# A fused normalisation, attention and 4-bit feed-forward kernel: unit 1's ramps moved into ScalarE's pauses, operand 6 made third, eight staging slots late in the first half, and ScalarE casting in the odd steps

## What is computed

```
q     = transpose(xn, (2, 0, 1))                       # 1024 positions, 4 x 1024
prob  = softmax(einsum('lnc,lmc->lnm', q, q) / sqrt(C))  # a 4 x 4 matrix for each position
s     = xn + transpose(einsum('lnm,lmc->lnc', prob, q))
gate  = xn @ Wg.T ; up = xn @ Wu.T                     # Wg, Wu: 2752 x 1024, 4-bit codes, a scale for every 64
g     = silu((silu(gate) * up) @ Wd.T)                 # Wd: 1024 x 2752
out   = x + s * g
```

## Time and profile before

| | |
|---|---|
| time, median of three runs | 2548.71 us |
| the profiled execution's own time | 2553.62 us |
| its span | 2551.5 us |
| TensorE (PE) busy, of the span | 2427.7 us, 95% |
| VectorE (DVE) busy | 1647.6 us, 65% |
| ScalarE (ACT) busy | 992.2 us, 39% |
| mean granted clock of TensorE | 0.978 of full |
| bytes by DMA, mean rate | 579.52 MB, 227 GB/s |

### The profile page before, as it was taken

The page is one execution under the profiler, slowest core; times in us unless marked ns, Lnnn a source line. Parts: engine busy times, 40 slices in busy tenths (PEclk is TensorE's granted clock), DMA queues, the critical chain, the costliest instruction groups (busy, mean ns, idle before and its releaser), DMA issues.

```text
span 2551.5 us, 30326 instructions
## 1 busy us (share of the span) xinstructions
PE 2427.7 (95%) x11214; PEld 1112.5 (44%) x11214; DVE 1647.6 (65%) x2866; ACT 992.2 (39%) x1261; POOL 84.1 (3%) x72
## 2 busy tenths in 40 slices
PE   2789999999999989999999999999999999999999
PEld 2334444444444434444444444444444444444444
DVE  8878887778988866787888886654532431431431
ACT  7776766766666434444455522111000001000001
POOL 0000000000000000000000000000011001011011
PEclk6889999999999999999999999999999999999999
DMA  7666665756656587655556654227876777777764
GB/s 249 214 192 219 212 200 197 225 168 235 232 193 221 183 318 242 225 180 198 194 197 203 215 182 154 106 79 284 349 281 274 302 290 287 276 280 291 313 261 161
DMA packets 171855, 579.52 MB, mean 227 GB/s; under 512 B 17632, under 2 KB 42896, under 8 KB 153916
## 3 DMA queue, kind: packets, MB, share of 16 engines
q1 hardware_dynamic: 136716, 289.21, 33.5%
q10 hardware_dynamic: 34992, 288.37, 30.0%
HBM read 388.76 MB, written 188.75 MB: 226 GB/s over the span
## 4 chain that ended last, share of the span: by engine, by line
PE 75%; DVE 10%; DMA 7%; issue 4%; ACT 2%; SPq 1%; POOL 0%; DVEq 0%; POOLq 0%; ACTq 0%
PE ps L1700 44%; PE ps L1846 30%; DMA arena<-xnsc 2%; DMA isc<-arena 2%; DVE arena L1325 2%; DMA arena<-in_x 2%; DVE arena L1204 1%; DVE arena L1318 1%; DVE arena L1229 1%; ACT arena L731 1%; PE ps L1657 1%; DVE arena L1495 0%; DVE arena L1490 0%; DMA xsc<-arena 0%; DVE arena L1253 0%
## 5 line engine op out<-in xcount | busy, mean ns | idle before, releaser
L1700 PE MATMUL ps<-arena 128*128 128x512 f16 x7152 | 1574.2, 383 | 67.8 <-DVE arena L1229 23.8
L1700 PEld LDWEIGHTS ps<-arena 128*128 128x128 f16 x7152 | 703.6, 99 | 925.7 <-issue 57.8
L1846 PE MATMUL ps<-arena 128*128 128x512 f16 x3696 | 797.9, 379 | 0.0
L731 ACT ACTIVATE arena<-arena,bias_t 128x1024 f32<-128x1024 f32 (+1 forms) x520 | 574.4, 1142 | 39.5 <-DMA arena<-in_gu 24.5
L1846 PEld LDWEIGHTS ps<-arena 128*128 128x128 f16 x3696 | 361.7, 98 | 436.1
L1325 DVE TENSOR_TENSOR arena<-arena 128x512 f16<-128x512 f32 x364 | 248.6, 684 | 22.5 <-ACT arena L884 20.7
L932 ACT ACTIVATE arena<-ps,gate_back 128x512 f32<-128x512 f32 x84 | 57.5, 684 | 370.2 <-PE ps L1700 370.1
L1116 ACT ACTIVATE arena<-arena,e_d 128x512 f32<-128x512 f32 x48 | 34.6, 721 | 424.3 <-DVE arena L1622 219.4
L1318 DVE CAST arena<-arena 128x512 f16<-128x512 f32 x336 | 137.0, 420 | 53.5 <-DMA isc<-arena 47.3
L696 POOL TENSOR_TENSOR arena<-arena 128x512 f32<-128x512 f32 x64 | 82.1, 1292 | 2454.3 <-DMA arena<-in_xt 2151.7
L942 ACT ACTIVATE arena<-arena,gate_back 128x512 f32<-128x512 f32 x84 | 60.5, 721 | 239.5 <-DVE arena L1492 231.0
(11 more groups left out here) (110 smaller groups left out, 1095.1 us busy)
## 6 DMA issues: line engine op xcount, KB each, us to landing
isc<-arena SPq DMA_DIRECT2D x308, 256.0 KB, 2.3
arena<-wdsc ACTq DMA_DIRECT2D x28, 2816.0 KB, 10.2
arena<-isc ACTq DMA_DIRECT2D x28, 2816.0 KB, 18.0
arena<-xnsc SPq DMA_DIRECT2D x48, 1024.0 KB, 10.8
wsc<-arena ACTq DMA_DIRECT2D x21, 1792.0 KB, 6.4
arena<-in_x SPq DMA_DIRECT2D x48, 512.0 KB, 6.0
arena<-in_gu ACTq DMA_DIRECT2D x43, 512.0 KB, 4.5
wdsc<-arena SPq DMA_DIRECT2D x77, 256.0 KB, 2.1
```

The source lines that it names most:

```text
L731: a_.activation(buf, src, ACT.Prelu, bias=bias_t[:, i:i + 1], scale=scale, alpha=alpha).then_inc(ramps, 1)
L1700: ins = t_.matmul(ps[:, bank, :], wreg[:, b, w, wa, k, :], xreg[:, j, o, k, xa, :], start=start and (k, wa, xa) == (0, 0, 0), stop=stop an ...
L1846: ins = t_.matmul(ps[:, bank, :], ring_w[b][:, k, wa, g, :], ring_i[b][:, k, xa, :], start=first and (k, wa, xa) == (0, 0, 0), stop=r not ...
```

## The change

1. `W_ORDER` becomes 0, 4, 5, 6, 1, 3, 2 (operand 6 third of the sums and fourth of the operands); the down weights keep the old order as `D_ORDER`. `W_CUT[13]` moves one low part from slot 2 to slot 1 and the two sums from slot 3 to slot 2.
2. Unit 1's 16 ramps: six before the first normalisations on ScalarE (three before), one behind them, one or three between the casts of blocks 0, 1 and 2, one before `p1_copy(0)` and three behind it. Unit 2's stand between the casts of blocks 4 to 7, with six in step 2; unit 3's are spread over steps 2 and 3 as 4 and 12.
3. VectorE makes unit 1's weights before `early_made(4)`, around the second half of step 0. Block 4's casts go from VectorE to ScalarE.
4. Steps 40 to 46 use eight staging slots; the four more lie in the memory of the x jobs' blocks and wait until the last x job is through.
5. In the odd steps 25 to 39 ScalarE does all seven casts of the job, of i jobs too, after `p1_copy` and the weight casts, and VectorE's items are the eleven `ACT_ITEMS`, none in slot 0.
6. `STAT_AT` puts 5, 1, 4 and 4 statistics into steps 4, 5, 6 and 7 (5, 0, 6, 3 before).

The diff holds, one after another, the tables, ScalarE's start, its steps, and VectorE's start. `early_highs(e, w, a, b)` now makes casts 0 and 1 of block e, then ramps a to b-1 of unit w, then the third cast. `c_high` is `x_high` for either kind of job.

```diff
-W_ORDER = [0, 4, 5, 1, 3, 6, 2]
+W_ORDER = [0, 4, 5, 6, 1, 3, 2]
+D_ORDER = [0, 4, 5, 1, 3, 6, 2]
...
-STAT_AT = {3: {0: 16, 3: 17}, 4: {0: 18, 1: 19, 2: 20, 3: 21, 4: 22}, 6: {k: 23 + k for k in range(6)}, 7: {1: 29, 2: 30, 3: 31}}
+STAT_AT = {3: {0: 16, 3: 17}, 4: {0: 18, 1: 19, 2: 20, 3: 21, 5: 22}, 5: {5: 23}, 6: {0: 24, 1: 25, 3: 26, 5: 27},
+           7: {0: 28, 1: 29, 3: 30, 5: 31}}
...
+ACT_JOB_AT = {s: jobs_at(s)[0] for s in range(24, 40) if PASS[s][1] and jobs_at(s)}
+ACT_JOBS = list(ACT_JOB_AT.values())
...
-RAMP_AT = {0: (1, 3, 16), 1: (2, 0, 16), 2: (3, 0, 8), 3: (3, 8, 16)}
+RAMP_AT = {2: (3, 0, 4), 3: (3, 4, 16)}
...
+MORE_AT = range(40, 47)
+for _n, _s in enumerate(STAGE_AT):
+    _k = 2 * NSLOT if _s in MORE_AT else NSLOT
+    SLOT.append((SLOT[-1] + 1) % _k if SLOT and SLOT[-1] + 1 <= _k else 0)
...
+ACT_ITEMS = ["t4", "t5", "l0", "l1", "l2", "l4", "t3", "l5", "t6", "l3", "l6"]
+ACT_CUT = [0, 0, 1, 2, 4, 7, 11]
-W_CUT = {5: [0, 0, 0, 1, 2, 3, 5], 8: [0, 0, 0, 1, 2, 3, 8], 13: [0, 0, 2, 3, 5, 5, 13], 4: [0, 0, 0, 0, 0, 0, 4],
+W_CUT = {5: [0, 0, 0, 1, 2, 3, 5], 8: [0, 0, 0, 1, 2, 3, 8], 13: [0, 0, 3, 5, 6, 6, 13], 4: [0, 0, 0, 0, 0, 0, 4],
...
-            for n in range(3):
+            for n in range(6):
                 ramp(1, n)
             for tt in (5, 6, 7):
                 normal(tt)
+            ramp(1, 6)
...
-            early_highs(0)
+            early_highs(0, 1, 7, 8)
...
-            ramps_of(0, 0, 1)
+            ramp(1, 12)
             p1_copy(0)
-            ramps_of(0, 1, 3)
+            w_high(1, 0)
+            for n in range(13, 16):
+                ramp(1, n)
             sil_a(0)
-            ramps_of(0, 3, 4)
-            ramps_of(1, 0, 1)
-            for o in W_ORDER:
+            for o in (4, 5, 6, 1, 3, 2):
                 w_high(1, o)
+            early_highs(4, 2, 0, 2)
             store_w(0)
-            early_highs(5)
+            early_highs(5, 2, 2, 4)
             p1_copy(1)
-            ramps_of(1, 1, 2)
-            early_highs(6)
+            early_highs(6, 2, 4, 7)
             sil_a(1)
-            early_highs(7)
-            ramps_of(1, 2, 4)
+            early_highs(7, 2, 7, 10)
...
-                if on_act:
-                    for o in (0, 1, 2):
-                        x_high(("x",) + XJOB_AT[s], o)
                 if s < TOTAL:
                     p1_copy(s)
+                if s == 2:
+                    for n in range(10, 16):
+                        ramp(2, n)
...
-                ramps_of(s, 0, 2)
+                if not job:
+                    ramps_of(s, 0, 2)
...
-                if on_act:
+                if job:
+                    for o in (0, 1, 2):
+                        c_high(job, o)
+                    ramps_of(s, 0, 3)
                     for o in (4, 5):
-                        x_high(("x",) + XJOB_AT[s], o)
+                        c_high(job, o)
...
+                if s == 3:
+                    w_high(2, 6)
                 if s > 2:
                     sil_a(s - 1)
...
+                if job:
+                    c_high(job, 3)
+                    ramps_of(s, 3, 4)
+                    c_high(job, 6)
+                else:
+                    ramps_of(s, 2, 4)
...
+            w_item(1, 0)
             first_half(0)
+            for i in (1, 2, 3, 4, 5, 6, 7, 9):
+                w_item(1, i)
+            for tt in (14, 15):
+                dve.wait_ge(xs_out[nat_slot(tt)], 16)
+            second_half(0)
+            for i in (8, 10, 11, 12):
+                w_item(1, i)
             early_made(4)
-            second_half(0)
-            for i in range(13):
-                w_item(1, i)
             early_made(5)
             first_half(1)
```

More of the change, by code:

```diff
@@ L80 @@
 XJOB_AT = {s: (2 + i // 4, i % 4) for i, s in enumerate([s for s in SPARE if s >= 24][-8:])}
-X_ACT = [XJOB_AT[s] for s in XJOB_AT if PASS[s][1]]
 GRAM_AT = {NSTEP + s: i for i, s in enumerate(SPARE[:16])}
@@ L111 @@
 JOB = {c: i for i, c in enumerate(JOBS)}
-CAST_HERE = {c: i for i, c in enumerate(c for c in JOBS if c[0] == "i" or c[1:] not in X_ACT)}
+ACT_JOB_AT = {s: jobs_at(s)[0] for s in range(24, 40) if PASS[s][1] and jobs_at(s)}
+ACT_JOBS = list(ACT_JOB_AT.values())
+CAST_HERE = {c: i for i, c in enumerate(c for c in JOBS if c not in ACT_JOBS)}
 NEARLY = 8
@@ L116 @@
 NG = len(EARLY_OPS)
-EARLY_HERE = [4]
-EARLY_ACT = [e for e in range(NEARLY) if e not in EARLY_HERE]
 NORM_DVE = [0, 1, 2, 3, 4, 8, 9, 10, 11, 14, 15] + list(range(16, 32))
@@ L164, with slot_uses @@
 NSLOT = 4
+MORE_AT = range(40, 47)
+STAGE_AT, SLOT, SLOT_USE = [], [], []
+for _s in range(TOTAL + 2):
+    for _n in range(sum(7 for _c in jobs_at(_s)) + (len(DOWN_OPS[DOWN_AT[_s][1]]) if _s in DOWN_AT else 0)):
+        STAGE_AT.append(_s)
+for _n, _s in enumerate(STAGE_AT):
+    _k = 2 * NSLOT if _s in MORE_AT else NSLOT
+    SLOT.append((SLOT[-1] + 1) % _k if SLOT and SLOT[-1] + 1 <= _k else 0)
+    SLOT_USE.append(SLOT[:-1].count(SLOT[-1]))
+def slot_uses(k, last):
+    return SLOT[:last + 1].count(k)
 JOB_CUT = [0, 3, 6, 9, 12, 15, 18]
 JOB_ITEMS = ["h0", "h1", "l0", "t4", "h2", "l1", "t5", "h4", "l2", "h5", "l4", "t3", "l5", "t6", "h3", "l3", "h6", "l6"]
+ACT_ITEMS = ["t4", "t5", "l0", "l1", "l2", "l4", "t3", "l5", "t6", "l3", "l6"]
+ACT_CUT = [0, 0, 1, 2, 4, 7, 11]
 SOON_CUT = [0, 8, 13, 18, 18, 18, 18]
-W_CUT = {5: [0, 0, 0, 1, 2, 3, 5], 8: [0, 0, 0, 1, 2, 3, 8], 13: [0, 0, 2, 3, 5, 5, 13], 4: [0, 0, 0, 0, 0, 0, 4],
+W_CUT = {5: [0, 0, 0, 1, 2, 3, 5], 8: [0, 0, 0, 1, 2, 3, 8], 13: [0, 0, 3, 5, 6, 6, 13], 4: [0, 0, 0, 0, 0, 0, 4],
          9: [0, 0, 0, 0, 0, 0, 9], 1: [0, 0, 0, 1, 1, 1, 1], 0: [0] * 7}
@@ L266, in build @@
         stage = [carve(210 + 2 * i, 2, F16).rearrange("p (s t) -> p s t", s=2) for i in range(NSLOT)]
+        stage += [carve(176 + 2 * i, 2, F16).rearrange("p (s t) -> p s t", s=2) for i in range(NSLOT)]
         n0 = 126 * 256
@@ L347, in build @@
         c_lo = sem("c_lo")
-        st_out = [sem(f"st_out{i}") for i in range(NSLOT)]
+        st_out = [sem(f"st_out{i}") for i in range(2 * NSLOT)]
         codes_in = sem("codes_in")
@@ L603, in _ @@
                     if not g:
-                        sp.wait_ge(c_lo, JOB["x", 3, 3] * 7 + 7)
+                        for k in range(NSLOT, 2 * NSLOT):
+                            sp.wait_ge(st_out[k], 16 * SLOT.count(k))
                     else:
@@ L779, in load_xb @@
                 last = STAGED["x", 2 + j, 3, o]
-                for k in range(NSLOT):
-                    act.wait_ge(st_out[k], 16 * ((last - k) // NSLOT + 1))
+                for k in range(2 * NSLOT):
+                    if slot_uses(k, last):
+                        act.wait_ge(st_out[k], 16 * slot_uses(k, last))
                 act.dma_start(xreg[:, j, o, :, :, :], xsc[j, o, :, :, :, :]).then_inc(xb_in[j][o], 16)
@@ L964, in _, with early_highs @@
                 normal(tt)
-            def early_highs(e):
-                for g in range(NG):
-                    early_high(e, g)
+            ramp(1, 6)
+            def early_highs(e, w, a, b):
+                early_high(e, 0)
+                early_high(e, 1)
+                for n in range(a, b):
+                    ramp(w, n)
+                early_high(e, 2)
             early_evac(0, (0,))
@@ L980, in _ @@
                 w_high(0, o)
+            ramp(1, 8)
             early_high(1, 2)
@@ L987, in _ @@
             early_high(2, 1)
-            for o in (1, 3, 6, 2):
+            for o in (6, 1, 3, 2):
                 w_high(0, o)
+            for n in range(9, 12):
+                ramp(1, n)
             early_high(2, 2)
@@ L1048, in _ @@
                 if 4 <= s < 40 and u + 1 != LAST:
-                    for o in ([0, 4, 5], [1, 3, 6, 2])[j]:
+                    for o in ([0, 4, 5], [6, 1, 3, 2])[j]:
                         w_high(u + 1, o)
@@ L1420, in background @@
                 for c in jobs:
-                    at = SOON_CUT if c[0] == "x" and c[1:] not in X_ACT else JOB_CUT
+                    at = ACT_CUT if c in ACT_JOBS else SOON_CUT if c[0] == "x" else JOB_CUT
                     for i in range(at[slot], at[slot + 1]):
```

75 lines of the change are left out of this document (35 added, 40 removed).

## The result

The changed kernel takes 2522.14 us, the median of four runs (2519.10 to 2523.32); the kernel before, run beside it, takes 2547.34 (2544.99 to 2553.59). The ratio is 0.9895 with a 95% interval of 0.9875 to 0.9916: 25 us faster by the medians, 27 by the ratio. The forecast of 2506 was 16 us too low. The result lies inside the range of 2492 to 2528, but outside the likeliest case's own 2496 to 2514. It is 4 us above the 2518.6 and 2518 of the first two rivals, and came about by the mechanism of neither.

A forecast was written before the change was run, and what follows sets the result against it. TensorE was taken as the bound nearly everywhere, VectorE in steps 24 to 39. Terms 20.5 - 1.7 + 5.9 + 13.2 + 6.4 - 1.0 = 43.3 us off the 2548.7 median gave 2505.4, stated as 2506; range 2492 to 2528.

The forecast's parts named there:

- likeliest case: The forecast itself for the whole kernel: 2496 to 2514 us, chance 0.46.
- start to p7 of step 4: Kernel start: earlier ramps and weights let TensorE begin step 4 at 156.7, not 177.19; gain 20.5 us.
- step 5's give-back: Step 5: VectorE runs close behind TensorE, c21 comes about 183.8 against p7 at 182.1; 1.7 us given back.
- statistics, up to p7 of step 7: Step 6: fewer statistics ahead of c21, so the 3.44 us wait and 2.5 of clock go; gain 5.9 us.
- steps 24 to 39: VectorE-bound rounds: ScalarE's casts shorten odd rounds, i by 2.7 and x by 1.2 us; gain 13.2 us in all.
- eight slots: Steps 40 and 41: VectorE's casts no longer wait for stores among the reloads, so c21 is on time; gain 6.4 us.
- reload: Wait at 952.46 for unit 0's reload: same bytes in less time, so 1.0 us more waiting.
- The start's chain: Start up to step 4: step 1 begins without wait, p2 waits to 112.7, step 4 begins at 156.7.
- (1): Odd steps 24 to 39: late stores hold ScalarE and its SiLU, little or nothing won; 2518.6 us, chance 0.22.
- (2): Start: p2 of step 1 and blocks 6 and 7 cost 12 us more; 2518 us, chance 0.15.
- (3): Slower: SiLU so late in each of eight odd steps that the kernel loses; 2561 us at 7 late, chance 0.06.
- (4): All three places: waits only move and little is won; about 2545 us, chance 0.05.

## Why the forecast was right, and where it failed

The balance, in us by which TensorE is ahead of the kernel before at the same place, profile against profile (what the forecast called products in its counts of 84, 96 or 276 are single matmuls, 12 to each of p1 to p7):

| stretch | forecast | measured |
|---|---|---|
| start to p7 of step 4 | +20.5 | +14.8 |
| step 5's give-back | -1.7 | -1.5 |
| statistics, up to p7 of step 7 | +5.9 | -2.1 |
| from there to step 24 | 0 | -0.5 |
| steps 24 to 39 | +13.2 | +12.2 |
| eight slots | +6.4 | +6.3 |
| reload | -1.0 | -1.2 |
| the rest | 0 | +2.0 |
| sum | 43.3 | 30.0 |

How they are read. p7 of step 4: 177.19 against 155.47 and 24 matmuls more, 6.94 us by the row of the old order's run: 162.4. Step 5: 252 matmuls in 56.75 put its p7 at 196.1 before; after it is at 182.80, 13.3 ahead. Step 7: 237.37 against 226.18. Step 24: 557.52 against 546.80. Before the wait for c21 at 921.91: the kernel before stopped at 917.40 (921.91 less 4.51) with the matmul that the changed kernel passes at 894.5 (904.00 less 1.66 and 36 matmuls of 0.2164), 22.9 ahead. The end of the wait behind those 36 (1.66 in both): 933.20 before against 904.00, 29.2. Reload: 952.46 against 924.48, 28.0.

**The start's chain was right.** Step 1 begins without a wait; p2 of step 1 starts at 111.94 (112.7 forecast), step 1 ends at 122.3 (122.3), step 2's first half at 132.8 (134.9; it ran without the 2 us charged for blocks 7), step 4 begins at 155.47 (156.7).

**The step that failed there** is the sentence "TensorE's p1 of step 4 starts at 156.7, not 177.19". The row at 177.19 is not p1. Before the run of 96 stands p1 of step 3, which the rows did not show:

```profile
140.15 2.75 PE L1700 MATMUL ps<-arena 128*128 128x512 f16 x12
```

The run of 96, from p6 of step 3 at 146.53, is then the 72 that are left of step 3's first and step 2's second half, and 24 more: p1 and p6 of step 4. p7, which waited for operand 6, sixth in the old order, came at 177.19. I compared p1 after with p7 before, 24 matmuls apart, 5.2 us at full clock and 6.94 as they ran. p1 itself came 1.2 early, at 155.47, which leaves the 5.7 us missing in that row of the table. The count told it: 12 and 96 are 108 matmuls, where I took 84. The forecast's own upper bound, 240 products to 146.1, did count to p7.

**The statistics failed.** "That block comes at about 183.8" was right: p7 of step 5 waited 0.89, to 182.80. "The wait of 3.44 and 2.5 of clock go: 5.9" was wrong. The wait became 6.95. I counted how many statistics stood before c21, and miscounted: of the six in step 6 the last stands in slot 5, behind c21, so five were ahead of it before. Of the changed table's, three in step 6 and one at the end of step 5 lie between that c21 and the one before it: four for five. And I took their loads to be in when VectorE came earlier. The load of tile 26 is asked for behind four scale loads and took 13.77 us; the load that ended the wait of 4.26 before took 7.79. What the runs show is this much: of seven profiled executions with new table and new order and without the later statistics, all wait, 4.6 to 7.1 us; with one tile moved behind c21 two of two do not; with the new table and the old order one does not; with the old table and new order one of two waits; with both old, one does not. So both the number of tiles ahead of c21 and the time that the last load takes matter. Why that load takes 13.77 us was not isolated: scale loads, a load of codes and a weight store lie beside it, and the one profile in which the codes came behind it had 8.4.

With the measured values put in for these two terms the sum is 43.3 - 5.7 - 8.0 = 29.6, against 30.0; the other terms are off by no more than 1.0 each, and 2.0 of the 30.0 lie in no term. The forecast also took its sum, made from an execution 4.9 above the median of three, off the median itself. By the medians the gain was 25.2, and part of the miss of 16 lies there.

**Steps 24 to 39 were right in sum (12.2 for 13.2), by parts partly.** The odd i rounds are 21.7, 21.6 and 20.4 us against 24.15, 22.7 and 23.7: 2.3 less on average, 2.7 forecast. The odd x rounds are 24.1, 22.4 and 23.4 against 22.9, 24.7 and 24.8: 0.8 less, 1.2 forecast. VectorE's cycle from round 26 to 30 was 79.3, above the 76 to 78 of the forecast and just inside its limit of 79.5; the next two were 77.4 and 77.5, where 80.9 and 81.9 were before. The late engine is ScalarE's SiLU, as forecast, for 13.2 us in five waits. For the i half, the run with its casts taken back is 9.35 us slower by the medians (3 x 2.7 and 1.5 forecast), but in its profile, the fastest of six, only 3.6 of that are seen. How the 12.2 divide between i and x rounds is open. The upper bound's 27.9 is 28.2 by the forecast's own numbers (863.20 less 835.0); nothing was added up from it.

**Eight slots** were right, by the profile (6.3) and by the run without them (5.05 by the medians, 7.2 from the wait on in its profile).

**The clock.** The 2 us charged for each wait above 2 us is too regular. After 1.81 us 168 matmuls take 36.43, no loss, as forecast; but after 3.09 us 168 take 36.43 too, while after 3.61 us 336 take 75.65, 3.0 more than in the row at 546.80.

**The rivals.** (1) ScalarE held: from 560 to 900 its casts wait for i stores three times, 9.7 us in all, 3.9 the longest, and for x stores four times, 5.0 in all. Steps 24 to 39 won their 12.2 all the same. (2) The start hands its gain on: its number nearly came true (2518 for 2522), its place not, since p2 of step 1 and blocks 6 and 7 were on time; what was missing lay in the counting at step 4 and in the statistics up to step 7. (3) and (4) fell. That the range held is partly luck: it did so because it reached to the rivals, not because the term that failed had wide bounds: I gave the statistics 0 to 5.9 and they were -2.1.

**Left open.** The profiles with the wait at step 7 reach step 24 later than all those without it (543.7 to 546.8 against 538.3 to 542.4). In the whole time it is likely and not settled: the old table (0.9871) and the later one (0.9872) each overlap the changed kernel's interval. What makes the load long, and how much each kind of odd round won, are open too.

## What to carry to other kernels

Before a row of a timeline is taken as a milestone, count the matmuls since the last known one and say which product it is: an error of 24 matmuls cost 5.7 us of the forecast here, and the durations around it were right to 2.1. When an edit brings an engine forward, look at each load that it will meet and ask what releases that load; one that stands in a queue behind others may take twice its usual time (here 13.77 us, where 6.2 is the median), and the wait that was to go may grow. Count the instructions between two milestones by the order in which the engine runs them, slot by slot, and not by step. When two engines and one load share a round, moving one engine's work first shifts the wait to the next; here the SiLU first gained about 7 us, and moving the sums as well gained nothing. And before one profile is taken to explain a difference of medians, see where it lies among its kernel's runs: the one that gave 3.6 us for 9.35 was the fastest of six.
